# Reordering ScalarE's evictions and operand splits in a batched low-rank-update linear layer

## The reference, cut to what matters

```python
z1 = jnp.einsum('bfi,bir->bfr', x, v[:, 0]) / inch
z = jnp.einsum('bfr,bor->bfo', z1, u[:, 0]) / r      # u = v = the side input, rank 16
y = jnp.einsum('bfi,oi->bfo', x, W) + fc_bias + z + b
return x + jax.nn.gelu(y, approximate=False)
```

## Time and profile before

| what | value |
|---|---|
| median of 3 runs | 398.92 us (398.77 to 401.34) |
| the profiled execution, its own time | 398.59 us |
| span of the profiled execution | 396.8 us |
| TensorE matmul busy | 384.8 us |
| VectorE busy | 294.2 us |
| ScalarE busy | 201.2 us |

### The profile page before, as it was taken

One profiled execution on the slowest core, in us unless ns is written; L12 is line 12 of the kernel. 1 busy time (PEld: TensorE's weight loads), 2 busy tenths in 40 slices (PEclk: granted clock), 3 DMA queues, 4 the chain that ended last, 5 costly groups with the idle time before them and its releaser, 6 DMA issues.

```text
span 396.8 us, 7835 instructions
## 1 busy us (share of the span) xinstructions
PE 384.8 (97%) x3065; PEld 305.0 (77%) x3065; DVE 294.2 (74%) x188; ACT 201.2 (51%) x214; POOL 0.7 (0%) x5
## 2 busy tenths in 40 slices
PE   8998999999999999999999999999999999999995
PEld 3676888777877777877777787777787777788874
DVE  3579787777797777798777788777779777779852
ACT  3367246654446664445665444665444666444542
POOL 0000000000000000000000000000000000000000
PEclk9999999999999999999999999999999999999999
DMA  7778888887667877666877666777666787766123
GB/s 195 219 177 268 256 247 235 269 263 239 197 207 211 264 209 245 212 197 214 247 211 251 217 194 220 228 229 238 235 192 216 212 254 217 241 199 201 72 115 133
DMA packets 27756, 85.75 MB, mean 216 GB/s; under 512 B 6832, under 2 KB 6960, under 8 KB 23776
## 3 DMA queue, kind: packets, MB, share of 16 engines
q1 hardware_dynamic: 27088, 84.41, 69.2%
q10 hardware_dynamic: 656, 1.18, 1.0%
HBM read 35.75 MB, written 33.55 MB: 175 GB/s over the span
## 4 chain that ended last, share of the span: by engine, by line
PE 68%; ACT 17%; SPq 5%; issue 4%; DMA 4%; DVE 1%; ACTq 1%; DVEq 0%
PE y L413 65%; ACT w_high L244 12%; SPq L175 5%; ACT result L290 4%; DMA f_stack<-f_parts 2%; DMA base_w<-w_t 1%; PE y L405 1%; DVE w_low L305 1%; PE y L401 1%; PE y L397 1%; PE update L482 1%; ACTq L290 1%; SPq L161 0%; ACTq L284 0%; SPq L189 0%
## 5 line engine op out<-in xcount | busy, mean ns | idle before, releaser
L413 PE MATMUL y<-x_high,w_high 64*128 64x512 f32 x928 | 185.3, 394 | 3.9 <-ACT result L290 2.4
L413 PE MATMUL y<-x_low,w_high 64*128 64x512 f32 x928 | 182.5, 387 | 0.0
L290 ACT ACTIVATE result<-y,bias 128x512 f32<-128x512 f32 x128 | 81.0, 687 | 174.5 <-PE y L413 166.1
L305 DVE TENSOR_TENSOR w_low<-full_w,w_high 128x2048 fp32r<-128x2048 f32 (+1 forms) x38 | 74.3, 1955 | 79.5 <-ACT w_high L244 79.1
L413 PE MATMUL y<-x_high,w_low 64*128 64x512 f32 x928 | 124.7, 387 | 0.0
L413 PEld LDWEIGHTS y<-x_high,w_high 64*128 64x128 f32 x928 | 88.2, 184 | 32.0 <-ACT result L290 13.5
L413 PEld LDWEIGHTS y<-x_high,w_low 64*128 64x128 f32 x928 | 88.2, 185 | 17.4
L413 PEld LDWEIGHTS y<-x_low,w_high 64*128 64x128 f32 x928 | 88.5, 185 | 16.3
L348 DVE TENSOR_TENSOR result<-result,x_in 128x1024 f32<-128x1024 f32 (+1 forms) x65 | 78.0, 1201 | 6.0 <-ACT result L290 6.0
L309 DVE SCALAR_TENSOR_TENSOR full_w<-update,base_w 128x2048 f32<-128x2048 f32 (+1 forms) x38 | 74.0, 1947 | 9.0 <-DMA base_w<-w_t 6.7
L305 DVE TENSOR_TENSOR x_low<-x_in,x_high 128x2048 fp32r<-128x2048 f32 (+1 forms) x38 | 74.0, 1946 | 5.0 <-ACT x_high L253 5.0
(11 more groups left out here) (15 smaller groups left out, 29.7 us busy)
## 6 DMA issues: line engine op xcount, KB each, us to landing
out_t<-result SPq DMA_DIRECT2D x63, 512.0 KB, 3.4
x_in<-x_t SPq DMA_DIRECT2D x31, 1024.0 KB, 6.3
f_stack<-f_parts SPq DMA_DIRECT2D x186, 64.0 KB, 4.0
f_stack<-f_parts SPq DMA_DIRECT2D x124, 32.0 KB, 3.8
x_in<-x_t ACTq DMA_DIRECT2D x4, 256.0 KB, 9.1
base_w<-w_t SPq DMA_DIRECT2D x4, 256.0 KB, 8.1
f_parts<-factors SPq DMA_DIRECT2D x1, 896.0 KB, 7.1
out_t<-result SPq DMA_DIRECT2D x2, 256.0 KB, 2.5
```

The lines of the kernel that those rows point to most:

```text
L290: nc.scalar.activation(result[j % SLOTS][:, m, :], y[m][:, :], ACT.Gelu, bias=bias[:, bass.ds(b * CHUNKS + m, 1)]).then_inc(gelu_ready, 1)
L305: nc.vector.tensor_tensor(out, whole, high.bitcast(fp32), ALU.subtract).then_inc(ready, 1)
L413: return nc.tensor.matmul(y[m][:, :], w[rows, c, m * P:(m + 1) * P], x[rows, c, :], start=first, stop=last)
```

## The change

ScalarE's order per batch becomes: gelus of tiles 2 and 3 of batch b-1 (where that batch is a halves batch), `split_x` of b+1, `split_w` of b+1, gelus of tiles 0 and 1 of b. For the batches that go whole (0, 1 and 31) all four gelus stay in their own step. The gelu with its waits is now a function of its own. Nothing changes on the other engines; VectorE's use of `previous_batch` is only another way to write the same indices.

```diff
+        def previous_batch(t, j):
+            return (t, j - 1) if j else (t - 1, UNROLL - 1)
...
+            def gelu(t, j, m):
+                b = UNROLL * t + j
+                act.wait_ge(y_ready, CHUNKS * b + (m if is_whole(t, j) else m // TILES * TILES + 1) + 1)
+                if m == 0 and not (isinstance(t, int) and b < SLOTS):
+                    act.wait_ge(stored[j % SLOTS], 2 * 16 * (UNROLL // SLOTS * t + j // SLOTS))
+                if m == 0 and is_first(t, j):
+                    act.wait_ge(bias_ready, 1)
+                nc.scalar.activation(result[j % SLOTS][:, m, :], y[m][:, :], ACT.Gelu,
+                                     bias=bias[:, bass.ds(b * CHUNKS + m, 1)]).then_inc(gelu_ready, 1)
...
+                tp, jp = previous_batch(t, j)
+                if not is_first(t, j) and not is_whole(tp, jp):
+                    for m in range(TILES, CHUNKS):
+                        gelu(tp, jp, m)
                 if piecewise(tn, jn):
                     for c in range(CHUNKS // 2):
                         high_pieces(b + 1, c)
                 elif not is_last(t, j):
                     split_x(tn, jn)
-                    if piecewise(t, j):
-                        split_w(tn, jn)
-                for m in range(CHUNKS):
...
-                    if m == 0 and not is_last(t, j) and not piecewise(t, j):
-                        split_w(tn, jn)
+                    split_w(tn, jn)
+                for m in range(CHUNKS if is_whole(t, j) else TILES):
+                    gelu(t, j, m)
```

More of the change, by code:

```diff
@@ L352, in finish_previous @@
                 if not is_first(t, j):
-                    tp, jp = (t, j - 1) if j else (t - 1, UNROLL - 1)
-                    add_x(tp, jp, slice(HALF, CHUNKS))
+                    add_x(*previous_batch(t, j), slice(HALF, CHUNKS))
                 if j == 1 and not (isinstance(t, int) and t == GROUPS - 1):
```

## The result

The changed kernel took 387.28 us in the median of 4 runs (385.23 to 387.81), the kernel before 398.85 us (4 runs): a ratio of 0.969 (95% interval 0.964 to 0.973). It is 3.1% faster; the forecast was 386.2 us in a range of 384.5 to 390.

What follows compares the result with a forecast made beforehand. TensorE's own order, 97% busy, was taken to bound the kernel through its small gaps. Gelu waits (12.0 us) plus batch 31's first tile (0.6) made 12.7 us off 398.59: 385.9 profiled, 386.2 us median, range 384.5 to 390.

Steps and rivals of the forecast that it cites:

- The wait in every batch: TensorE's weight loads wait about 0.55 us per batch for ScalarE's gelu; removing this brings 12.0 us over 28 batches.
- the covers: On ScalarE, both gelu pairs end 1.6 us before TensorE wants them; gelus 0 and 1 behind w_high have 5.3 us.
- TensorE's own work per batch: Without the wait, a batch costs update 0.45 + phase 0 2.75 + other phases 8.16 = 11.36 us, against 11.79.
- my lower bound: TensorE's phase 0 takes 2.72 us like any other phase: 0.8 us better, 385.4 us.
- Rival 1: TensorE's slow phase 0 start stays because of gelus and VectorE beside it; only the idle gap goes: 389.8 us, chance 0.17.
- Rival 2: Denser neighbours slow TensorE throughout, giving the gap back: batch 11.75 us, 397.4 us in all, chance 0.05.
- Rival 3: On ScalarE, w_high holds back gelus 0 and 1 if over 5.3 us late; 6 us late gives 406.5 us, chance 0.03.
- 3.7 + 1.6 = 5.3 us of cover: ScalarE free 3.7 us before gelu 0 can start, plus 1.6 us before TensorE's next phase 0 wants the gelus.
- full_w has only an update ahead of it: On VectorE, full_w follows only the update, starting 0.77 us after it; the argument against gelus held behind w_high.
- Rival 4: Only weight loads fill TensorE, so pair distance shrinks to PEld's 77% busy share: about 323 us, chance 0.01.
- The ends: Start-up unchanged for TensorE; batch 31's first tile falls from 3.31 to 2.72 us, 0.6 us more gain; tail as before.
- Up to 50.54 nothing is moved: In the start-up, up to 50.54 us, nothing that TensorE waits for is moved by the change.

Runs made afterwards that it cites:

- the kernel with the large copy: Changed kernel plus one spare ScalarE copy of 128x7168 elements between the w split and gelu 0 of every halves batch: 423.33 us, one run.
- The kernel with the late update: Changed kernel with batch 2's update moved behind its phase 0: 384.62 us (6 runs), ratio 0.964.

## Why the prediction was right, point by point

**The wait in every batch.** Right. The gelu waits are gone, and the covers came out as worked out: gelu 2 at 0.33 us after the update, gelu 0 at 9.01 (209.07; predicted 8.97), full_w at 0.82 (200.88; predicted 0.77).

**TensorE's own work per batch.** The term 11.36 measured 11.33: phase 0 takes 2.72, my lower bound, instead of batch 2's 2.75. Batch 2 was the wrong row to take: its update stands behind a wait of its own, 1.55 us for the factors, so its phase 0 had part of the slow start. This brought 12.73 us instead of 12.08.

**Rival 1, the slow start of phase 0 due to its neighbours.** Out. In the changed kernel gelus 2 and 3 (200.39 to 201.66) and full_w (from 200.88) run beside phase 0 (from 200.51), and it keeps the pace; in the kernel with the large copy, where TensorE waits for a gelu again, phase 0 takes 2.85 to 2.90 again. The slow start goes with the break in TensorE's stream, not with the neighbours.

**Rival 2, denser neighbours.** Out: 0.227 us a pair with VectorE busy 81% of the middle.

**Rival 3, gelus held behind the splits.** Rightly judged as a mechanism that doesn't strike, but its threshold was mis-sized. The step "3.7 + 1.6 = 5.3 us of cover" took full_w as fixed to the update. It is tied to gelu 1 as well, through the addition ahead of it on VectorE, and the cover is 4.8 us. The wrong step was "full_w has only an update ahead of it". The price suffered with it: 6.06 us late should have cost 0.76 us a batch (6.06 less 5.3), and the period grew by 1.30.

**Rival 4, the weight loads as measure.** Out. The pairs' distance did not change. The Trainium skill (Perfetto Trace Analysis, section Identifying the Most-Contended Engine) takes the weight loads' busy share as a measure of headroom. By this trace it reads 86% in a stretch where no matmul waits for anything, so what is missing to 100% is no headroom here. It isn't even a fixed number: the second profile of the same kernel reads 94% in the same stretch, with the updates 11.33 us apart in both. The stretch from 100 to 200 us of the two (columns as above):

```profile
100.00:200.00 100.00, 100.00 (x886) 85.66 (x884) 81.19 (x47) 54.67 (x54) 0.00 (x0) 1.00 0.76 234
...
100.00:200.00 100.00, 100.00 (x885) 94.41 (x884) 80.51 (x47) 54.34 (x56) 0.00 (x0) 1.00 0.75 231
```

**The ends.** Batch 31's first tile took 2.87, not 2.72: 0.15 us missed. Its first matmul is followed after 0.33 us and the next ones come up to 0.24 us apart, as behind a gap, though the list has no wait of a matmul there. The kernel with the late update does the same at the change from whole to halves (37.24, phase 0 at 2.88). Why TensorE breaks off at such a change is not shown. "Up to 50.54 nothing is moved" was true and still missed the point. The median is 1.1 us above the forecast, since three of its four runs had the lower mean clock, and the one run of the kernel before that I reckoned from had not. Of the runs of the changed kernel with the lower clock only one has a trace, and it lost the clock in batch 2. I had no term for this; that the median still lies in the range is owed to the upper end, which was set for rival 1. At the full clock the changed kernel takes 385.2 to 386.1 us, which holds the 385.9 that I worked out for the profiled execution.

**What stays open.** The changed kernel had the lower clock in 7 of 10 runs, the kernel before in 8 of 22. That is too few to say that the change makes it more frequent, and no mechanism for it was tested; the runs of the kernel before that had it lost about 3 us, not 2, and have no trace here.

## What to carry to other kernels

Find the instruction that stands between two others that are ready together, and ask how early it could run: here one split placed ahead of a pair of gelus gave 3%, while the same split placed behind the pair cost 4%. When an in-order engine gets a new order, write it as a ring over all batches: that shows what really moved, and the cover is then the period less the longest ring, through the other engines too. A forecast made from one execution inherits its luck, so look for a gap in the start-up whose after-effect could differ from run to run.

## What the runs showed of the hardware that I had not expected

TensorE's granted clock fell behind an idle gap in batch 2 in some executions. From 40 to 44 us its mean was 0.58, and within that it stood at 0.50, the lower of the two levels (1.2 of 2.4 GHz), while TensorE was busy; pairs came every 0.43 us instead of 0.227. The Trainium skill (TensorE: Matmul & The Clock Gate, section What's actually happening) describes this as a gate that is released by activity and closes when the engine has been idle; the trace agrees in kind. The length of the gap alone did not decide: in the profiled runs waits of 1.50, 1.55, 1.59 and 2.38 us kept the clock, one of 2.24 lost it, and so did 3.06 us in the kernel with the large copy and 3.18 in the one with the w split behind gelu 1. Filled with 1.9 us of matmuls on zeros, the same place kept it in six runs of six.

The other surprise is the restart after a gap. The first pair took 0.33 us to the next instead of 0.227 and those behind it up to 0.24, so that a wait of some 0.3 us between two matmuls cost 0.15 us on top of itself. The length of the wait mattered little: behind one of 1.00 us, in the kernel with the large copy, phase 0 took 2.87 us, and at the change of form in the late-update kernel, where the distance between two starts was 0.31 instead of 0.227, it took 2.88.
